# Grouped convolutions in three float16 products instead of float32: image halves formed on GpSimd, expert rows and weights loaded in a new order

## What is computed

```python
def gn(v, groups=32): ...            # per image and group: (v - mean) / sqrt(var + eps)
def layer0(x):                       # mixture of convolutions, 8 channel groups of 16
    stats = concat(mean, std)                        # router input, per image
    topk_p, topk_i = top_k(softmax(softmax(stats @ router_w.T)), 2)
    shared = silu(group_norm(conv1x1(x, shared_w)))  # "y0"
    # two chosen experts, 3x3, grouped: "y1" and "y2"
    expert = sum(rw[k] * silu(group_norm(conv3x3(x, fused_w[topk_i[k]]))) for k in (0, 1))
    return shared + expert
def layer1(x):                       # window attention, 8x8 windows, 8 heads of 16
    q, k, v = qkv_w @ x + qkv_b
    o = softmax(q @ k.T / 4 + bias) @ v
    return proj_w @ (o + depthwise7x7(v_image)) + proj_b
x = x + layer0(gn(x)); out = x + layer1(gn(x))
```

## Time and profile before

| quantity | value |
|---|---|
| time, median of 3 runs | 763.06 us (760.45 to 766.43) |
| time of the profiled execution | 761.66 us |
| its span (first to last instruction) | 759.7 us |
| mean granted PE clock | 0.963 of full speed |
| busy PE / DVE / ACT / POOL | 645.3 / 565.1 / 453.1 / 188.5 us |

### The profile page before, as it was taken

How to read it: one execution, slowest core, us unless ns; L and a number is a source line. 1 busy time by engine, 2 the same in 40 slices (tenths; PEclk the granted TensorE clock), 3 DMA queues, 4 the chain that set the end, 5 groups by cost and what they waited for, 6 DMA issues and landing times.

```text
span 759.7 us, 18623 instructions
## 1 busy us (share of the span) xinstructions
PE 645.3 (85%) x6926; PEld 388.0 (51%) x6926; DVE 565.1 (74%) x1124; ACT 453.1 (60%) x758; POOL 188.5 (25%) x295
## 2 busy tenths in 40 slices
PE   5426759899989899999999899999999898889892
PEld 3412324655556464656555565646566566444430
DVE  3842656888888888988888888889888977332692
ACT  1123555768676776867686767768676852355451
POOL 4042133140404223131404042231312101000182
PEclk9997868999999999999999999999999999999997
DMA  8433183555646574746556464747452242465194
GB/s 329 180 132 98 59 223 108 174 158 153 184 129 200 145 206 147 213 128 200 160 151 189 128 199 144 215 138 210 134 168 86 82 147 72 139 222 181 20 257 167
DMA packets 53871, 121.13 MB, mean 159 GB/s; under 512 B 10131, under 2 KB 26646, under 8 KB 53782
## 3 DMA queue, kind: packets, MB, share of 16 engines
q1 hardware_dynamic: 41814, 78.87, 32.9%
q0 software_dynamic: 8800, 28.45, 15.3%
q10 hardware_dynamic: 3168, 12.62, 4.3%
HBM read 70.58 MB, written 40.93 MB: 147 GB/s over the span
## 4 chain that ended last, share of the span: by engine, by line
PE 47%; ACT 25%; issue 12%; DVE 6%; DMA 5%; POOL 1%; ACTq 1%; POOLq 1%; SPq 0%; DVEq 0%
PE g L1067 10%; PE g L1085 7%; ACT y L518 6%; PE t L1135 4%; PE g L1095 4%; PE g L1263 4%; ACT vp L563 4%; PE pv L1150 4%; PE s L1124 3%; PE s L1254 3%; DMA vt<-x 3%; ACT y L514 3%; ACT pt L584 3%; PE t L1254 3%; ACT L518 2%
## 5 line engine op out<-in xcount | busy, mean ns | idle before, releaser
L1067 PE MATMUL g<-xsh,wsel 96*128 96x512 f32 x256 | 132.6, 647 | 23.8 <-ACT y L514 13.1
L514 ACT ACTIVATE y<-g 128x512 f32<-128x512 f32 x96 | 55.6, 596 | 92.0 <-PE g L1067 75.6
L875 DVE TENSOR_REDUCE mx<-s 128x8 f32<-128x512 f32 x128 | 87.0, 679 | 26.8 <-PE s L1124 26.8
L811 DVE BATCH_NORM_STATS2 st<-y 128x6 f32<-128x512 f32 x96 | 64.6, 686 | 51.7 <-ACT y L514 51.6
L1135 PE MATMUL t<-ident,less 128*128 128x128 f32 x512 | 79.3, 278 | 15.7 <-ACT pt L584 15.0
L879 DVE TENSOR_TENSOR less<-s,mx 128x512 f32<-128x512 f32 x128 | 88.5, 691 | 4.4
L1067 PEld LDWEIGHTS g<-xsh,wsel 96*128 96x128 f32 x256 | 46.7, 200 | 76.3 <-issue 63.8
L1135 PEld LDWEIGHTS t<-ident,less 128*128 128x128 f32 x512 | 62.5, 145 | 44.7 <-DVE less L879 21.7
L584 ACT ACTIVATE pt<-t 128x512 f32<-128x512 f32 x128 | 74.6, 595 | 14.2 <-PE t L1135 13.7
L1150 PE MATMUL pv<-vp,pt 128*64 128x34 f32 x2048 | 79.2, 222 | 3.0 <-DVE ot L893 2.8
L1150 PEld LDWEIGHTS pv<-vp,pt 128*64 128x64 f32 x2048 | 71.4, 140 | 4.0 <-ACT pt L584 2.9
(11 more groups left out here) (155 smaller groups left out, 1119.7 us busy)
## 6 DMA issues: line engine op xcount, KB each, us to landing
xsh<-xs POOLq DMA_DIRECT2D x64, 210.0 KB, 3.7
xs<-xn ACTq DMA_DIRECT2D x16, 578.0 KB, 2.9
vt<-x SPq DMA_DIRECT2D x4, 2048.0 KB, 17.6
xin<-x POOLq DMA_DIRECT2D x16, 512.0 KB, 4.7
sq_d<-qhl SPq DMA_DIRECT2D x32, 256.0 KB, 2.4
sk_d<-khl SPq DMA_DIRECT2D x32, 256.0 KB, 2.2
stack<-sk_d SPq DMA_DIRECT2D x64, 128.0 KB, 3.5
stack<-sq_d SPq DMA_DIRECT2D x64, 128.0 KB, 2.8
```

Source lines behind the costliest of these rows:

```text
L514: act.activation(y[:, k, h * HALF:(h + 1) * HALF], g[at][:, :], ACT.Identity).then_inc(g_free[at], 1)
L811: last = v.bn_stats(st[:, 2 * k + h, :], y[:, k, h * HALF:(h + 1) * HALF])
L875: v.tensor_reduce(mx[:, p % 2, :], scored, AX.X, ALU.max).then_inc(sem["s_max"], 1)
L1067: last = mm(g[at][:, :], wsel[:, k - 1, C * dy:C * dy + C], xsh[:, k - 1, dy + 16 * h:dy + 16 * h + 16, 0:W], start=(dy == 0), stop=(dy == 1))
```

## The change

1. Both operands of the convolutions become float16 pairs, high plus low, with a fixed scale (16 for the image, 64 for the weights) that `copy_y` takes out again. A product is high x high + high x low + low x high. y0 is three float16 matmuls for each half. For y1 and y2 the taps are laid out anew: `xa` (128 partitions) holds the three column shifts of the 16 channels in high (48), low (48) and the first two shifts in high again (32), `xb` (48) the third shift in high for three rows; `wsa` and `wsb` hold the matching weights. Each half takes three matmuls of 128 rows (one for each row of taps) and one of 48 rows, all float16.
2. The scaled float32 image is formed on POOL (`form_xn`, at the end of a turn, into `vn`), the high half on ACT (`high_xn`), the low half on POOL (`save_xn`), which also issues the DMA to `xs`; `xs` now has two slots.
3. POOL's `load_rows` is split: `load_weights` of both experts (two DMAs each), then the three-column `rsqrt`, then `load_rows` of both (four DMAs each). Each expert has its own semaphore, and `convolve` waits for its own expert alone.
4. The expert weights are split into halves on the chip, in the setup: one load on SP, three ACTIVATEs on ACT, two subtractions on POOL, and 32 DMAs on SP to scratch tensors in HBM (`save_experts`), which the first `load_weights` waits for.
5. DVE's `turn_v` stands in pair 6 instead of pair 7, and `x_coefs` ahead of pair 7's `maxima`. ACT's `high_xn` stands behind `copy_y` of y2 in pair 0 (before: `normalise` ahead of it), and `copy_y` of y1's second half ahead of `window` in pair 7.

```diff
+        xa = sb("xa", [C, TOP, H + 2, WPAD], F16)
+        xb = sb("xb", [SHR, TOP, H, WPAD], F16)
+        xhl = sb("xhl", [C, 2, H + 2, WPAD], F16)
...
+            sp.dma_start(wx32, wx).then_inc(sem["wx_loaded"], 16)
+            def save_experts():
+                sp.wait_ge(sem["wx_hi"], 2)
+                for copy in range(2):
+                    for e in range(E):
...
+                        sp.dma_start(dst, wxh[GC * e:GC * e + GC, :]).then_inc(sem["wx_saved"], 16)
...
+            def form_xn(j):
+                pool.wait_ge(xin_loaded[j % 2], 16 * (j // 2) + 16)
+                if j == 0:
+                    pool.wait_ge(sem["gn_scaled"], 1)
+                elif j >= 3:
+                    pool.wait_ge(sem["v_turned"], j - 2)
+                nc.gpsimd.tensor_scalar(vn[:, :], xin[:, j % 2, :], gnx[:, 0, j:j + 1], gnx[:, 1, j:j + 1],
+                                        ALU.mult, ALU.add).then_inc(sem["xn_full"], 1)
+            def save_xn(j):
+                pool.wait_ge(sem["xn_full"], j + 1)
+                pool.wait_ge(sem["xn_done"], j + 1)
+                nc.gpsimd.tensor_tensor(xhl[:, 1, 1:H + 1, 1:W + 1], vn[:, :].rearrange("p (y x) -> p y x", x=W),
+                                        xhl[:, 0, 1:H + 1, 1:W + 1], ALU.subtract).then_inc(sem["xn_low"], 1)
...
+            def load_rows(j, k):
...
+                wide = xa[:, k, :, :].rearrange("p h w -> p (h w)")[:, 0:RUN]
+                pool.dma_start(wide[0:SHR], rows(0, 1, 3, RUN)).then_inc(rows_loaded[k], 16)
+                pool.dma_start(wide[SHR:2 * SHR], rows(PADDED, 1, 3, RUN)).then_inc(rows_loaded[k], 16)
+                pool.dma_start(wide[2 * SHR:C], rows(0, 1, 2, RUN)).then_inc(rows_loaded[k], 16)
+                pool.dma_start(xb[:, k, :, :].rearrange("p h w -> p (h w)")[:, 0:RUN2], rows(2, WPAD, 3, RUN2)
+                               ).then_inc(rows_loaded[k], 16)
...
                 if has3:
-                    load_rows(b + 3)
+                    save_xn(b + 3)
+                    load_weights(b + 3, 0)
+                    load_weights(b + 3, 1)
                 if has2:
                     rsqrt(b + 2, 0, 3)
                 if has3:
+                    load_rows(b + 3, 0)
+                    load_rows(b + 3, 1)
                     choose_affine(b + 3)
...
                 else:
-                    pe.wait_ge(sem["rows_loaded"], 32 * TOP * (j + 1))
-                    pe.wait_ge(sem["chosen_w"], 16 * TOP * (j + 1))
+                    pe.wait_ge(rows_loaded[k - 1], ROW_DMAS * (j + 1))
...
                     if k == 0:
-                        last = mm(g[at][:, :], w[:, WSH:WSH + C], xn[:, 1 + 16 * h:17 + 16 * h, 1:W + 1], start=True,
+                        for part, (wpart, xpart) in enumerate(((0, 0), (0, 1), (1, 0))):
+                            last = mm(g[at][:, :], wsh[:, wpart, :], xhl[:, xpart, 1 + 16 * h:17 + 16 * h, 1:W + 1],
+                                      start=(part == 0), stop=(part == 2))
+                    else:
+                        for dy in range(3):
+                            mm(g[at][:, :], wsa[:, k - 1, C * dy:C * dy + C],
+                               xa[:, k - 1, dy + 16 * h:dy + 16 * h + 16, 0:W], start=(dy == 0), stop=False)
+                        last = mm(g[at][:, :], wsb[:, k - 1, :], xb[:, k - 1, 16 * h:16 * h + 16, 0:W], start=False,
                                   stop=True)
-                    else:
-                        for dy in range(2):
-                            last = mm(g[at][:, :], wsel[:, k - 1, C * dy:C * dy + C],
-                                      xsh[:, k - 1, dy + 16 * h:dy + 16 * h + 16, 0:W], start=(dy == 0), stop=(dy == 1))
```

172 lines of the change are left out of this document (111 added, 61 removed).

## The result

| | before | after |
|---|---|---|
| median of the runs | 763.34 us (760.45 to 766.43) | 725.95 us (724.16 to 730.35) |
| profiled execution | 761.66 us | 727.21 us |
| its span | 759.7 us | 725.5 us |
| mean granted PE clock | 0.963 | 0.965 |

The account below looks back on a forecast made before the run. PE bounded the 34.8 us turn; DVE would next, at 31.8. 13 turns x 3.0 = 39, plus 1 for turn 13 and 6 for setup, takes 46 off 761.66: 715.7, as median 717; range 707 to 740.

Parts of the forecast that it names:

- rival A: The forecast itself: DVE sets a turn of 31.8 us; 717 us, own range 708 to 727; chance 0.55.
- rival B: No single engine sets the turn; DVE keeps half its 3.3 us of waits, turn 33.1, time 734; chance 0.25.
- DVE's own need, 31.5: DVE's floor for a turn however fast PE becomes: 30.1 us busy plus 1.4 of gaps between short instructions.
- Step (a): Turn's boundary: DVE reaches q about 0.3 us too early for each half; 0.3 in all, ends 0 and 1.5.
- (c): Pair 7: DVE's wait for y1's second half goes, so its 2.0 us of waits for y count as gone.
- (b): Pair 4's exponential behind three silus and a table load: PE waits 1 to 2 us, covered by 2.8 of room.
- Price of a float16 matmul: PE's convolutions: 0.23 us per 512 columns, bounds 0.22 and 0.31; PE's turn falls from 32.7 to 28.7.
- POOL "all hidden": POOL's added work and DMA issues: 16.9 of 31.8 us busy, no bound; rows, load_x and one-column root in time.
- rival C: POOL's added elementwise work blocks DVE for its length, 3.6 us a turn; turn 35.4, time 764; chance 0.05.
- Setup: Ahead of the turns: image 0 and image 1 give 0, image 2 wins 5 to 8; together 6 us, -5 to +10.
- rival E: PE's bunched idle time lowers its clock; at 16 us of low clock a turn is 38.7, time 807; chance 0.05.

Follow-up runs that it names:

- f3: e2 with 20 idle float16 matmuls more on PE in each turn, their results overwritten; 761.69 us, ratio to before 1.000.
- g1: f1 with the 48-row matmul of each half of y1 and y2 left out; 713.96 us, ratio to before 0.935.
- e2: Changed kernel with DVE reading the attention outputs ahead of pair 7's maxima; 717.68 us, ratio to before 0.941.
- f1: e2 with POOL's three-column root ahead of the experts' weights, whose loads then alternate with the rows; 713.3 us, ratio to before 0.935.
- e4: Changed kernel with the 48-row matmul of each half of y1 and y2 left out; 733.41 us, ratio to before 0.960.
- e3: Changed kernel with DVE's transpose of v put back from pair 6 to the end of pair 7; 750.31 us, ratio to before 0.983.
- e1: Changed kernel with ACT's high_xn behind q's and k's high halves in pair 0 instead of ahead; 743.01 us, ratio to before 0.973.
- g3: f1 with DVE's transpose of v put back at the end of pair 7; 727.22 us, ratio to before 0.952.
- f4: Changed kernel with POOL issuing both experts' rows ahead of the three-column root; 821.48 us, ratio to before 1.078.
- g2: f1 with POOL's form_xn done three times instead of once from image 4 on; 716.38 us, ratio to before 0.939.

## Why the prediction came out as it did

The range held; the time was 9 us above the forecast. The changed kernel lies between rival A (717) and rival B (734): PE stopped being the bound, as both say, but DVE's waits are B's.

**DVE's own need, 31.5.** It was read too high. "The other 34.79 - 30.11 - 3.3 = 1.4 us are gaps" leaves out two waits of 0.2 that the same turn has (for `xr` and for k's high half), so the gaps were 1.0 and DVE's need 31.1. In the changed kernel it is 29.86 busy and 1.2 of gaps, 31.0. `f3` and `g1` show that PE stops deciding.

**Step (a), the waits of the turn: this is the step that failed.** "I take 0.3 in all, with 0 and 1.5 as ends": DVE waits 1.6 in each turn, 1.0 for q's high half, 0.3 for scores and 0.3 for `xr`. The last two were put at nothing without a reason: (c) speaks only of the waits for y, not of the 1.3 for scores in the earlier trace rows. 1.6 is also the figure of rival B. For q, I had compared ACT's order there before and after, and found the same total. What made it late was one step earlier: PE's product with v, held by DVE's outputs behind transpose, coefficients and maxima. `e2` puts a price of 0.87 on it. So the turn is 32.63 instead of 31.8: 1.3 more of waits, less 0.5 of need. Over 12 turns that is about 10 us, which with the long turn's 2.5 makes the 12.7 by which they pass 12 x 31.8 = 381.6. That `f1`'s turn of 31.77 meets the forecast of 31.8 is partly luck: need 30.9 and waits 0.9, against 31.5 and 0.3.

**Steps (b) and (c).** PE's wait for pair 4's exponential did not grow to 1 to 2 us; it is 0.7. DVE's waits for y are gone, as said.

**Price of a float16 matmul.** A half of y1 or y2 takes 0.27 for each matmul against 0.23 taken, inside 0.22 to 0.31. What the 0.23 left out goes with the matmul of 48 rows: where none follows, in `e4`, three take 0.66 us, 0.22 each. PE's turn without waits is 32.63 - 3.1 = 29.5 against 28.7. It cost nothing, being below DVE's. The Trainium skill (TensorE: Matmul & The Clock Gate, Back-to-back issue gap) gives about 216 ns isolated, and 131 ns sustained with weight loads; the 0.22 of `e4` agrees with the first, and nothing here came near the second.

**POOL "all hidden".** 16.49 busy against 16.9: right as a sum. The place was seen for the rows and not for the root, which had only 1.2 us to spare behind two weights' DMAs. In ten turns of twelve it holds; the root is 1.4 late in the first turn and 1.5 in the long one. It also made `e3` slow, and `e1` in part.

**Contention (rival C).** Its price, 3.6 us a turn, did not come: in the changed kernel's ordinary turns DVE's rows are as long as before. But its mechanism is real, and the argument against it looked at the wrong instructions: the step for q was compared, and of DVE's two-input instructions only the large sums in pairs 4 and 5 were named, not the small ones on statistics (L885, L888), which stand near POOL's new work. The rule of the Trainium skill (SBUF — State Buffer, SBUF: two separate sides) on a lock between GpSimd and DVE agrees with the trace: L888 took 2.01 us instead of 0.16 at 87.78, and L885 took 0.57 in the turns of `g3`, each ending with POOL's subtraction. In ordinary turns the subtraction ends at 216.62 and L885 starts at 219.39, so 2.8 us keep them apart, which the prediction had not looked at. No run put POOL's work beside the large sums, so for those it stays open.

**Setup.** 6.0 us against 6 by the row of `high_xn`, 7.0 by DVE's first step for q. The pieces do not all agree. y1 of image 0 starts at 60.60 (62 forecast, 58.92 before), and its 16 instructions take 5.7 us instead of 9.7, so they end 2.3 earlier where 0 was taken. y1 of image 2 starts at 107.47 instead of 112.20, still at the lower level (granted 0.50), and takes 3.9 instead of 7.1: 7.9 us won by its end, inside the 5 to 8.

```profile
60.60 1.46 PE L1163 MATMUL g<-xa,wsa 128*128 128x512 f16 x3 [4.65 <-DMA xb<-xs]
```

**The clock (rival E).** It stayed at 1.00 in ordinary turns. Its mechanism is real all the same: in the long turn PE stood 2.39 us at the loop's place and what came behind ran slow, three matmuls taking 1.39 instead of 0.75; a root 1.5 late went with a turn 2.5 longer. `e1`, `e4` and `f4` show it too.

```profile
343.17 0.70 PE L1248 MATMUL pv<-vp,pt 128*64 128x34 f32 x16 [2.39 <-DVE ot L988]
```

**What stays open.** Why POOL stood 3.60 us before one issue; why the clock fell behind some waits of 2.1 us and not behind others; the 5.2 us of `g3` behind its turns; and whether a turn below 31.6 is to be had, since no run took work off DVE.

## What to carry to other kernels

When the bounding engine gets faster, the next one's own need plus its gaps is the floor, and that part could be foretold to half a microsecond (count every wait of that engine before calling the rest gaps); what was not read off the old profile were the new loops, and for those one asks of each instruction that is moved what stands behind it on its own engine, and follows that through the other engines until it returns. An in-order queue of an engine that is half idle still decides when a small result stands in it behind a long row of DMA issues: put the small one first. A wait that costs nothing by itself may still cost the clock behind it, a second engine's elementwise work has to be checked against each instruction that it can meet and not only against the long ones, and an edit that helps in one order can hurt in another, so it is tried in the kernel that it is meant for.

## What the runs showed of the hardware

- Less PE work made a kernel slower: `e4`, 733.4 against 726.0 us. At one place PE stood 1.83 to 2.87 us in each turn; the 6 us behind it were granted 0.72 seven times, 0.50 once and 1.00 four times. Of two waits of 2.11 us one was followed by 1.00 and one by 0.72, so the length of the wait alone does not decide. Behind 1.09 of idle time, at the same place in the changed kernel, it was 1.00; behind 4.73 (`f4`) 6 us were granted 0.81.
- POOL's subtraction (two inputs in SBUF, 2.06 us) held up a small DVE instruction with two inputs in SBUF until it ended: 2.01 us instead of 0.16 at 87.78 and 0.89 at 121.53 in the changed kernel, 0.57 in the turns of `e3` and `g3`. A POOL tensor-scalar of 1.19 us, done three times over, did not lengthen what DVE did beside it (`g2`: 29.78 against 29.79 us a turn).
- The float16 matmul of 512 columns costs 0.22 us where only 128-row ones stand in the half (`e4`), 0.27 on average in a half with one of 48 rows, and half of a float32 one is 0.455: 2.1 or 1.7 to 1 for each instruction.
- POOL's issue gap ahead of the weights' DMAs was 0.64 to 1.39 us, and once 3.60.
